# An attention kernel whose TensorE signals scores, projections and value chunks through its next maxima matmul

## What is computed

```python
Q, K, V = (split_heads(x @ W.T + b) for W, b in ((Wq, bq), (Wk, bk), (Wv, bv)))
tQ, tK = (split_heads(cond[:, None] @ W.T + b) for W, b in ((Wq, bq), (Wk, bk)))
scores = einsum('bhqd,bhkd->bhqk', Q + tQ, K + tK) / sqrt(32)
out = einsum('bhqk,bhkd->bhqd', softmax(scores), V)
return x + out            # heads merged again
```

## Time and profile before

| | us |
|---|---|
| median of three runs (lowest, highest) | 656.06 (655.94, 656.4) |
| span of the profiled execution | 654.2 |
| TensorE busy | 647.3 (99%) |
| VectorE busy | 540.6 (83%) |
| GpSimd busy | 487.4 (74%) |
| ScalarE busy | 389.6 (60%) |
| one stage in the middle (stage 13 to stage 14) | 19.75 |

### The profile page before, as it was taken

How to read it: one execution, slowest core, us unless ns; L and a number is a source line. 1 busy time by engine, 2 the same in 40 slices (tenths; PEclk the granted TensorE clock), 3 DMA queues, 4 the chain that set the end, 5 groups by cost and what they waited for, 6 DMA issues and landing times.

```text
span 654.2 us, 10054 instructions
## 1 busy us (share of the span) xinstructions
PE 647.3 (99%) x3528; PEld 442.8 (68%) x3528; DVE 540.6 (83%) x815; ACT 389.6 (60%) x684; POOL 487.4 (74%) x204
## 2 busy tenths in 40 slices
PE   9999999999999999999999999999999999999997
PEld 6776677666677666676666776666776666776542
DVE  5776888888888888888888888888888888888787
ACT  6455666565566565666556665556665555564773
POOL 6338877778877779777779777779777788666992
PEclk9999999999999999999999999999999999999999
DMA  8944333555333555333554434553434544424501
GB/s 260 255 97 115 103 107 87 143 147 140 97 110 94 144 147 132 97 108 103 146 146 125 104 96 114 146 147 107 116 90 127 146 131 124 119 67 110 151 18 65
DMA packets 48038, 79.87 MB, mean 122 GB/s; under 512 B 9458, under 2 KB 9714, under 8 KB 47986
## 3 DMA queue, kind: packets, MB, share of 16 engines
q1 hardware_dynamic: 47632, 79.07, 45.1%
q10 hardware_dynamic: 356, 0.16, 0.1%
HBM read 19.95 MB, written 8.39 MB: 43 GB/s over the span
## 4 chain that ended last, share of the span: by engine, by line
PE 95%; DVE 2%; issue 1%; ACT 1%; DMA 1%; ACTq 0%; POOLq 0%; DVEq 0%
PE bank L350 27%; PE bank L442 18%; PE bank L420 18%; PE bank L462 16%; PE bank L398 14%; DVE bank L737 1%; PE bank L368 1%; ACT Pt L637 1%; DMA Qs<-mt 1%; DVE part_sums L762 0%; DVE rr L786 0%; DVE ends L807 0%; PE bank L470 0%; DVE rr L775 0%; DVE bank L793 0%
## 5 line engine op out<-in xcount | busy, mean ns | idle before, releaser
L637 ACT ACTIVATE Pt<-bank 128x512 f32<-128x512 f32 x512 | 299.2, 600 | 216.3 <-PE bank L442 144.8
L737 DVE TENSOR_REDUCE mf<-bank 128x1 f32<-128x512 f32 x496 | 332.6, 686 | 72.3 <-PE bank L420 69.3
L943 POOL TENSOR_TENSOR A<-A,Pt 128x2048 f32<-128x2048 f32 x59 | 270.9, 4592 | 4.6
L442 PE MATMUL bank<-Qs,Ks 98*128 98x512 f32 x496 | 197.5, 404 | 1.4 <-DMA Qs<-mt 1.4
L420 PE MATMUL bank<-Ks,Qs 96*128 96x512 f32 x496 | 197.6, 399 | 0.2
L943 POOL TENSOR_TENSOR A<-Pt 128x2048 f32<-128x2048 f32 x30 | 138.4, 4614 | 9.3 <-DVE part_sums L762 9.3
L442 PEld LDWEIGHTS bank<-Qs,Ks 98*128 98x128 f32 x496 | 93.1, 188 | 52.1 <-ACT Pt L637 25.9
L462 PE MATMUL bank<-Pt,V 128*32 128x512 f32 x1024 | 118.9, 596 | 0.0
L913 POOL TENSOR_TENSOR Xl<-xr,Xh 128x512 fp32r<-128x512 f32 x28 | 36.1, 1291 | 110.0 <-ACT Xh L598 110.0
L420 PEld LDWEIGHTS bank<-Ks,Qs 96*128 96x128 f32 x496 | 93.8, 189 | 26.7 <-DVE bank L737 3.0
L350 PE MATMUL bank<-Xh,Wl 128*128 128x512 f32 x256 | 102.2, 399 | 0.0
(11 more groups left out here) (73 smaller groups left out, 389.4 us busy)
## 6 DMA issues: line engine op xcount, KB each, us to landing
Qs<-hi SPq DMA_DIRECT2D x60, 256.0 KB, 3.6
Ks<-hi SPq DMA_DIRECT2D x60, 256.0 KB, 3.6
Qs<-lo SPq DMA_DIRECT2D x30, 256.0 KB, 4.1
Ks<-lo SPq DMA_DIRECT2D x30, 256.0 KB, 3.4
xr<-xT SPq DMA_DIRECT2D x28, 256.0 KB, 2.7
res<-xT SPq DMA_DIRECT2D x28, 256.0 KB, 2.9
outT<-ot SPq DMA_DIRECT2D x28, 256.0 KB, 3.1
Qs<-mt SPq DMA_DIRECT2D x122, 4.0 KB
```

Source lines behind the costliest of these rows:

```text
L442: e.matmul(st_bank(u)[:, :], k[0:98, j, kc * P:(kc + 1) * P], q[0:98, j, :], start=True, stop=True).then_inc(t_st, 1)
L637: e.activation(exponentials(g)[:, kc, j, :], st_bank(u)[:, :], ACT.Exp, scale=SCALE).then_inc(a_e, 1)
L737: e.reduce_max(to[:, 4 * j + qc:4 * j + qc + 1], MXB[u % 2][:, :], AXX).then_inc(v_mx, 1)
L943: e.tensor_tensor(sums, ex[:, 0, :, :] if kc == 1 else sums, ex[:, kc, :, :], ALU.add).then_inc(p_a, 1)
```

## The change

No instruction is moved, added or removed on TensorE but for its signals. 616 of its 1280-odd increments are dropped:

- the score of a slot that has a maxima matmul (465 of 512) no longer increments; its consumers wait for `t_mx` of the first maxima matmul behind it in the same slot. The other 47 scores count `t_st` as before;
- the last matmul of a projection of group 3 and later (87) no longer increments; it is told by the next score or maxima matmul that increments. In stages 1 to 24 that is the maxima matmul of the next slot, since the next score has no increment any more;
- of the four chunks of values only the first and the last increment (64 fewer).

The tables of slots, the order of every engine and all sizes stay. The diff, cut to its core:

```diff
+        told_by, plain, u = [], 0, OPENING
+        for t in range(G):
+            for n in range(SLOTS):
+                if maxima_at(t, n):
+                    told_by.append((t_mx, u + 1))
+                    u += maxima_at(t, n)
+                else:
+                    plain += 1
+                    told_by.append((t_st, plain))
+
+        def scored(u):
+            return told_by[u]
+
+        def projection_done(kind, g):
+            if g >= NSLOT:
+                return told[(kind, g)]
+            return (t_vj, g + 1) if kind == "v" else (t_pj, 2 * g + "qk".index(kind) + 1)
+
+        def values_done(g, kc=KC - 1):
+            return 2 * g + (1 if kc == 0 else 2)
...
+            untold = []
+
+            def tell(signal, count):
+                for use in untold:
+                    told[use] = (signal, count)
+                untold.clear()
+
+            def projected_all(m, use, signal):
+                if use[1] < NSLOT:
+                    m.then_inc(signal, 1)
+                else:
+                    untold.append(use)
...
                 if n == 11:
-                    m.then_inc(t_vj, 1)
+                    projected_all(m, use, t_vj)
...
                 e.matmul(MXB[u % 2][:, :], q[0:96, j, qc * P:(qc + 1) * P], k[0:96, j, :],
                          start=True, stop=True).then_inc(t_mx, 1)
+                tell(t_mx, u + 1)
...
-                e.matmul(st_bank(u)[:, :], k[0:98, j, kc * P:(kc + 1) * P], q[0:98, j, :],
-                         start=True, stop=True).then_inc(t_st, 1)
+                m = e.matmul(st_bank(u)[:, :], k[0:98, j, kc * P:(kc + 1) * P], q[0:98, j, :],
+                             start=True, stop=True)
+                if not maxima_at(g, n):
+                    m.then_inc(t_st, 1)
+                    tell(*scored(u))
...
-                    m.then_inc(t_pv, 1)
+                    if kc in (0, KC - 1):
+                        m.then_inc(t_pv, 1)
...
-                e.wait_ge(t_vj, g + 1)
+                e.wait_ge(*projection_done("v", g))
...
-                    e.wait_ge(t_pv, KC * before + kc + 1)
+                    e.wait_ge(t_pv, values_done(before, kc))
...
-                e.wait_ge(t_st, u + 1)
+                e.wait_ge(*scored(u))
```

More of the change, by code:

```diff
@@ L208, in cond_attention @@
         turns = {}
+        told = {}
         AHEAD = {("q", 1): STB[0], ("k", 1): STB[1]}
@@ L352, in project_qk @@
                 if n == 11:
-                    m.then_inc(t_pj, 1)
+                    projected_all(m, use, t_pj)
             def weights_wait(qk, c, i):
@@ L595, in x_hi @@
                 if b >= 2 and kc == 0:
-                    e.wait_ge(t_pj, 2 * KC * (b - 1))
-                    e.wait_ge(t_vj, KC * (b - 1))
+                    for kind in "vqk":
+                        e.wait_ge(*projection_done(kind, KC * (b - 1) - 1))
                 e.activation(Xh[:, b % 2, kc, :], xr[:, n % 2, :], ACT.Copy).then_inc(a_x, 1)
@@ L605, in qk_hi @@
                 b, c = divmod(g, KC)
-                e.wait_ge(t_pj, 2 * g + qk + 1)
+                e.wait_ge(*projection_done("qk"[qk], g))
                 if qk == 0 and g == 0:
@@ L616, in v_copy @@
                 b, c = divmod(g, KC)
-                e.wait_ge(t_vj, g + 1)
+                e.wait_ge(*projection_done("v", g))
                 if b >= 2 and c == 0:
-                    e.wait_ge(t_pv, KC * KC * (b - 1))
+                    e.wait_ge(t_pv, values_done(KC * (b - 1) - 1))
                 e.activation(V[:, b % 2, c, :], ring_bank(("v", g))[:, :], ACT.Copy).then_inc(a_v, 1)
@@ L625, in exps @@
                 if n == 0 and g == G - 3:
-                    e.wait_ge(t_pj, 2 * G)
+                    e.wait_ge(*projection_done("q", G - 1))
+                    e.wait_ge(*projection_done("k", G - 1))
                 elif j == 0 and g >= 1 and g != G - 3:
                     before = g - 1 if g < G - 3 else g - 2
-                    e.wait_ge(t_pv, KC * before + kc + 1)
+                    e.wait_ge(t_pv, values_done(before, kc))
                     e.wait_ge(p_a, 3 * before + max(kc, 1))
@@ L791, in normalised @@
                 e.wait_ge(v_f, finished(g, 2))
-                e.wait_ge(t_pv, KC * (g + 1))
+                e.wait_ge(t_pv, values_done(g))
                 e.tensor_tensor(O[:, :], O[:, :], rr[:, :], ALU.mult).then_inc(v_f, 1)
@@ L930, in add @@
                 if kc == 1 and g == G - 4:
-                    e.wait_ge(t_pv, KC * (G - KC))
+                    e.wait_ge(t_pv, values_done(G - KC - 1))
                 elif kc == 1 and g == G - 3:
-                    e.wait_ge(t_vj, G)
+                    e.wait_ge(*projection_done("v", G - 1))
                 elif kc == 1 and g == G - 2:
@@ L1000, in stack @@
                 if g >= NSLOT and g != G - 4 and qk == 0:
-                    e.wait_ge(t_st, SLOTS * (stack_before(g) + 1))
+                    e.wait_ge(*scored(SLOTS * (stack_before(g) + 1) - 1))
                 e.wait_ge(a_hi, 2 * g + qk + 1)
@@ L1079, in sync_program @@
                 if t == G - EARLY:
-                    e.wait_ge(t_pj, 2 * (G - KC))
-                    e.wait_ge(t_vj, G - KC)
+                    for kind in "qkv":
+                        e.wait_ge(*projection_done(kind, G - KC - 1))
                     e.dma_start(Xl[96:98, 0, :, :].bitcast(F32), Ks[96:98, 0, :, :].bitcast(F32)).then_inc(d_ks, 16)
```

## The result

The changed kernel takes 676.24 us (median of five runs, 675.94 to 676.51), beside 656.34 us for the kernel before on the same chip: a ratio of 1.0301, with a 95% interval of 1.0290 to 1.0313. The forecast was 674.4 us in a range of 670 to 680. It is 19.9 us slower, where 18.3 were forecast.

A forecast was written before the change was run, and what follows sets the result against it. TensorE, busy 647.3 of 654.2 us, was taken as the bound. The later value projection's 17.5 us plus 0.8 us at the end made 18.3, added to 656.06 for 674.4 us, range 670 to 680.

The forecast's parts named there:

- TensorE's stream is the bound: Whole kernel: TensorE is busy 647.3 of 654.2 us, so every nanosecond its stream loses or saves is the kernel's.
- An increment costs nothing: TensorE's stream: dropping 616 increments gains nothing; a small gain of 1 ns each would be 0.6 us.
- the first rival: TensorE's stream gets faster without the increments: 15.6 us gained, time 658.8 us; chance of a time under 654.7: 0.03.
- The 7 ns a step: Matmul steps in the stages are 7 ns longer than before the stages, kept as the far end of a gain.
- The later value projection: Slots 5 to 7, stages 1 to 24: copy 0.94 us later, score 7 loses 0.73 us, 17.5 us in all.
- Exponentials a matmul later: Slots 13 to 15 and the next stage's first two: scores told 0.23 us later, taken as 0, at most 1.4 us.
- The other signals: Later signals for query and key copies, middle value chunks and SyncE's waits: priced at nothing.
- The end: From stage 25: three or four places each take the full 0.23 us, 0.8 us, between 0 and 2.
- The rival of a second stall in each stage: Slots 13 to 15: three scores lose 0.13 us each, 9.4 us in all, time 683.8 us; chance 0.06.

The follow-up runs named there:

- the middle chunks alone: The kernel before, with only the two middle chunks of values losing their increment: 656.26 us beside 656.17, ratio 1.0000.
- the last kernel: The changed kernel, value copy moved behind exponential 6, scores of slots 13 to 15 and stages 25 to 30 signalling themselves: 656.19 us beside 656.12, ratio 1.0009.
- the run of score 14 alone: The kernel before, with only the score of slot 14 of stages 1 to 24 told by its maxima matmul: 657.90 us beside 655.95, ratio 1.0029.
- the run of the last stages alone: The kernel before, with only the scores of stages 25 to 30 told by a maxima matmul: 656.77 us beside 655.95, ratio 1.0011.

## Why the prediction was right, and where it was off

- *TensorE's stream is the bound.* Right. Every loss in it came out at the end: 19.5 us up to the start of stage 25, 0.6 us behind it and 0.1 us before the first score make the 20.2 us by which the spans differ.
- *An increment costs nothing.* Right, and the first rival is out: 1056 more of them moved the time by -0.13% to +0.05%, and 64 or 475 fewer (the middle chunks alone, and the last kernel) brought nothing. The 7 ns a step on which the rival rested stay when every matmul of that stretch increments. (In the earlier trace rows three of the 27 matmuls increment, the last of them at 16.93, where the forecast counted two; the argument does not hang on it.) The rule of the Trainium skill that was set beside it, TensorE: Matmul & The Clock Gate, "The cost: per-tile semaphore tail", would give the 1056 increments 27.8 us as an estimate; the trace does not agree for a stream of full-width matmuls. The Trainium skill states this for tiled matmuls of which each one increments, and no run here has that case.
- *The later value projection.* Right in mechanism, place, count and size. Forecast: copy 0.94 us later, exponential 5 with it, score 7 late by 0.73 us, 24 times, 17.5 us. Measured: 0.94 us, 0.73 us in the stage shown, 24 times, in sum 15.3 + 2.5 = 17.8 us. Four runs carry it: with the 29 signals back the loss goes; with the signal 0.24 us sooner it shrinks by just that; with the copy out of the way it goes though the signal stays late; and the copy's move is worth nothing alone. The choice of the earlier trace rows for the distance from a late weight load to its matmul after a standstill was the one that mattered, and it held.
- *Exponentials a matmul later.* The mechanism was right, the size was not: this is the term that failed. I took 0 and 1.4 us as its upper end; it measured 1.8 us in the trace and 1.95 us in the run of score 14 alone. I had worked out the room for score 15 from the earlier trace rows and taken it for all three scores there. Scores 15 and 1 lose 0.02 us a stage or less, as said. The gap between exponential and weight load was indeed the same for all three in the kernel before, 0.13 to 0.15 us. But the load of score 0 needs 0.11 us behind its exponential and the others 0.05, so score 0 has 0.06 us less room, and 0.08 us are lost there in each of 24 stages (2 to 25). The gap of a place that does not wait could not show this. A place of the same kind that does wait could, and the trace of before has one at 610.13 us, in stage 29.
- *The other signals.* Right: the middle chunks alone changed nothing, and the last kernel, in which the query's and key's signals are still late, has no loss left in its trace.
- *The end.* Forecast 0.8 us between 0 and 2, measured 0.8 us by the run of the last stages alone and 0.6 us in its trace. The agreement owes something to luck: I counted three or four places of 0.23 us, and there are nine of 0.07 to 0.16 us, less two that give time back.
- *The rival of a second stall in each stage* has a part of the truth: there is a second loss in each stage, though in slot 0 rather than in slots 13 to 15, and at a fifth of its price. Its mechanism is out: it needed a matmul 0.23 us behind its late load, and score 0 comes 0.04 us behind (343.84 to 343.88).

So the forecast was short by the term of the exponentials. In the traces, 20.2 us stand against 18.3: 1.8 us for the exponentials and 0.3 for the value projection more than forecast, 0.2 less at the end. The medians differ by 19.9 us, 1.6 more than forecast. The 0.3 us between the two counts are less than what runs of one kernel differ by.

## What to carry to other kernels

A signal that is free where it is given has a price where it is late. Before a signal is moved to a later instruction, ask of each waiter what stands behind it on its engine and who waits for that: here ScalarE was 60% busy, and a copy that nobody missed held back an exponential with 0.12 us of room. Where such a late wait can't be avoided, it belongs behind the work that others wait for.

Read the room at every place that repeats in another setting, the first slot of a stage above all. The gap in a place that does not wait is not yet the room. Look also for a place with the same waits that does stand still, and see how soon it starts there: here 0.11 us for score 0 and 0.05 us for the others made all the difference.

## What the runs showed that was not expected

- A late weight load costs the stream nothing until it is some 0.1 us late: score 0's load comes 0.19 us late and 0.08 us are lost. This room comes on top of the wait's own, which at score 7 is 0.12 us of gap less the 0.05 us that the load needs. So the copy could be 0.21 us late.
- When a matmul's weight load is late by a little, the loss is not in its own start but in the start of the next: score 0 is recorded in time, 0.47 us long, and the maxima matmul behind it 0.31 us later in place of 0.23. Where only the value copy was told 0.23 us late, 1.0 of the 1.2 us stand behind score 7 and 0.1 us ahead of it. A look at start times of the waiting matmuls alone misses most of it.
